# A Perceiver block on one core: the attention's output is regrouped without transposes and divided on its regrouped rows, sums and norms become stages of their own, and the last down product is made of two fp32r products

## The reference

```python
dot = jnp.einsum('bhsd,bhtd->bhst', Q, K) / np.sqrt(D_HEAD)
scores = jax.nn.softmax(dot, axis=-1)
out = jnp.einsum('bhst,bhtd->bhsd', scores, V)
out = out.reshape(B, T_src, D_MODEL)          # (head, s, d) as it lies: a row of 256 is 16 values of s of one head
return out @ Wh.T + bh
...
x = x + xattn(layernorm(x), ctx, ctx)
x = x + attn(layernorm(x))                    # divided by max(den, 1e-06)
x = x + ffn(layernorm(x))                     # silu(gate) * up, then down; weights are int32 / 127
```

## Time and profile before

| | |
|---|---|
| runs | 875.84, 876.47, 878.09 us (median 876.47) |
| profiled execution | 875.48 us, its span 873.8 us, so 1.7 us lie around the span |
| TensorE busy | 829.1 us (95%) |
| ScalarE, VectorE busy | 541.5 us (62%), 417.2 us (48%) |
| granted TensorE clock, mean | 0.99 of full |
| last batch's tail, alone at the end | from 796.97 us of the span on |

### The profile page before, as it was taken

One profiled execution on the slowest core, in us unless ns is written; L12 is line 12 of the kernel. 1 busy time (PEld: TensorE's weight loads), 2 busy tenths in 40 slices (PEclk: granted clock), 3 DMA queues, 4 the chain that ended last, 5 costly groups with the idle time before them and its releaser, 6 DMA issues.

```text
span 873.8 us, 20543 instructions
## 1 busy us (share of the span) xinstructions
PE 829.1 (95%) x8817; PEld 569.8 (65%) x8817; DVE 417.2 (48%) x746; ACT 541.5 (62%) x598; POOL 47.1 (5%) x76
## 2 busy tenths in 40 slices
PE   6899999999999998999999998999999999989876
PEld 5666666666666666676666665667666666657656
DVE  7433236444644445534654446354474444402654
ACT  2478887776577665667567764575657666672141
POOL 1034000000000000000000000000000000000010
PEclk9899999999999999999999999999999999999999
DMA  7486654646344333346343441443614333202000
GB/s 248 172 258 237 241 183 166 209 158 193 122 146 146 142 125 133 122 133 191 136 146 145 146 142 53 158 158 129 195 65 170 122 122 119 100 2 50 0 2 15
DMA packets 58768, 120.08 MB, mean 137 GB/s; under 512 B 21552, under 2 KB 29744, under 8 KB 55152
## 3 DMA queue, kind: packets, MB, share of 16 engines
q1 hardware_dynamic: 56880, 114.31, 38.3%
q0 software_dynamic: 1792, 4.40, 1.7%
HBM read 78.84 MB, written 37.75 MB: 133 GB/s over the span
## 4 chain that ended last, share of the span: by engine, by line
PE 82%; DVE 8%; issue 4%; DMA 2%; ACT 2%; DVEq 1%; POOL 1%; SPq 0%; POOLq 0%; ACTq 0%
PE ps_o L816 26%; PE ps_s L828 18%; PE ps_pa L662 10%; PE ps_pa L617 10%; PE ps_pa L763 2%; PE ps_pa L692 2%; PE ps_pa L788 2%; PE ps_pa L775 2%; PE ps_pa L754 1%; ACT probs L1258 1%; PE ps_pa L740 1%; DMA oscr<-y 1%; PE ps_pa L684 1%; PE ps_pa L795 1%; PE ps_pa L767 1%
## 5 line engine op out<-in xcount | busy, mean ns | idle before, releaser
L1258 ACT ACTIVATE probs<-ps_s 128x1024 f32<-128x1024 f32 x512 | 496.8, 1023 | 234.2 <-PE ps_s L828 227.7
L816 PE MATMUL ps_o<-probs,values 128*17 128x256 f32 x4096 | 256.1, 385 | 0.0
L828 PEld LDWEIGHTS ps_s<-qstack,kstack 64*128 64x128 f32 x2048 | 140.0, 186 | 99.6 <-ACT probs L1258 48.8
L828 PE MATMUL ps_s<-qstack,kstack 64*128 64x256 f32 x2048 | 194.0, 307 | 5.3 <-ACT probs L1258 5.3
L816 PEld LDWEIGHTS ps_o<-probs,values 128*17 128x17 f32 x4096 | 104.1, 98 | 98.7 <-issue 9.8
L1343 DVE TENSOR_SCALAR kparts<-ps_pa,b_heads 128x512 fp32r<-128x512 f32 x64 | 48.0, 750 | 107.4 <-PE ps_pa L617 107.1
L662 PE MATMUL ps_pa<-wv_hi,ctx_hi 128*128 128x256 f32 x256 | 79.6, 311 | 2.9 <-DVE wv_lo L1331 2.2
L1360 DVE TENSOR_TENSOR values<-ps_pa,bv_pair 128x512 f32<-128x512 f32 x64 | 44.2, 690 | 77.5 <-PE ps_pa L662 77.1
L662 PE MATMUL ps_pa<-wv_lo,ctx_hi 128*128 128x256 f32 x256 | 72.5, 283 | 0.0
L662 PE MATMUL ps_pa<-wv_hi,ctx_lo 128*128 128x256 f32 x256 | 72.4, 283 | 0.0
L617 PE MATMUL ps_pa<-ctx_hi,wk_hi 128*128 128x512 f32 x128 | 56.4, 441 | 0.0
(11 more groups left out here) (274 smaller groups left out, 786.7 us busy)
## 6 DMA issues: line engine op xcount, KB each, us to landing
kstack<-kscr SPq DMA_DIRECT2D x96, 512.0 KB, 5.3
kscr<-kparts SPq DMA_DIRECT2D x64, 512.0 KB, 2.7
ctx_raw<-ctxT SPq DMA_DIRECT2D x32, 512.0 KB, 6.5
qstack<-qscr SPq DMA_DIRECT2D x12, 256.0 KB, 3.5
qscr<-qparts SPq DMA_DIRECT2D x4, 512.0 KB, 3.1
xh<-x SPq DMA_DIRECT2D x4, 256.0 KB, 5.4
kstack<-kstack SPq DMA_DIRECT2D x2, 512.0 KB, 6.0
qstack<-ksample SPq DMA_DIRECT2D x4, 256.0 KB, 3.6
```

The source lines that it names most:

```text
L816: last = mm(ps_o[32 * j:32 * j + DH + 1, g * S:(g + 1) * S], values[par][:, i, head_of_step(g, j), :], prob[:, j * S:(j + 1) * S], start=b ...
L828: last = mm(ps_s[s % 2][:, j * S:(j + 1) * S], kstack[par][rows, u, i * P:(i + 1) * P], queries[rows, u, :], start=True, stop=True)
L1258: nc.scalar.activation(probs[n % AHEAD][:, :], ps_s[n % 2][:, :], ACT.Exp, scale=float(DH) ** -0.5).then_inc(fast["exp_done"], 1)
```

## The change

1. `o` alone is left on the way: `write_heads` writes each of the four 17-partition pieces of o_sb to memory by a DMA of its own (rows of 1 KB, denominators too), with no transpose before it. `read_rows` reads them back in pieces of 64 bytes as rows of 16 successive s of one head, all 17 of them, into o_rows (a view of feat). A new VectorE stage `on` takes the reciprocals, checks the denominators and divides into y.
2. `ln1` and `ln2` are stages of their own, for VectorE alone: `wh` and `wout` give their signal behind the sum.
3. At the end two of the four writes are issued from ScalarE; the check of the denominators and its verdict stand later; `last_down` takes hid in two fp32r parts, which VectorE cuts (`cut`).
4. The down weights are held as fp32r; before the end they are read as fp32, as before. They are loaded by two DMAs.

```diff
-AT = {"o": 1, "oT0": 3, "oT1": 4, "yT": 12, "wh": 13, "ln1T": 19, ...
+AT = {"o": 1, "on": 9, "yT": 12, "wh": 13, "ln1": 13, "ln1T": 19, ...
-      ... "o2T1": 88, "y2T": 90, "wout": 92,
+      ... "o2T1": 88, "y2T": 90, "wout": 92, "ln2": 92,
...
-            "powered": (["ln0"], ["wh", "wout"]),
+            "powered": (["ln0"], ["ln1", "ln2"]),
...
-        oscr = scratch("oscr", [H, S, DH], FP32)
+        oscr = scratch("oscr", [ST, DH + 1, HALF, S], FP32)
...
+        def write_heads(eng, c, j):
+            t, e = j // CI, j % CI
+            eng.dma_start(oscr[t].rearrange("d (g e) s -> e d g s", e=CI)[e],
+                          o_sb[32 * j:32 * j + DH + 1, :, :]).then_inc(c["o_written"], 16)
...
-                wait_all((c["operand"], c.at("operand", clock, "oT1")))
-                for t in range(ST):
-                    sp.dma_start(oscr[:, t * P:(t + 1) * P, :].rearrange("h s d -> s h d"),
-                                 y[:, t, :].rearrange("p (h d) -> p h d", h=H)).then_inc(c["o_written"], 16)
+                wait_all((c["operand"], c.at("operand", clock, "o")))
+                for j in range(GH):
+                    write_heads(sp, c, j)
+            def read_rows(t, landed):
+                sp.dma_start(o_rows[:, t, :, :], oscr[t].rearrange("d h (a u) -> (h a) d u", u=DH)).then_inc(landed, 16)
             def regroup_output(c, tails):
-                wait_all((c["o_written"], tails * 32 + 32))
-                sp.dma_start(y[:, :, :], oscr.rearrange("(t a) (u s) d -> (a u) t (s d)", t=ST, u=S // DH)
-                             ).then_inc(c["o_in"], 16)
+                wait_all((c["o_written"], tails * (16 * GH) + 16 * GH))
+                for t in range(ST):
+                    read_rows(t, c["o_in"])
...
-            for t in range(ST):
-                sp.wait_ge(*vector_of(f"y{t}"))
-                sp.dma_start(oscr...)
-            sp.wait_ge(fast["o_written"], B * 32)
+            sp.wait_ge(*vector_of("o0"))
+            sp.wait_ge(*scalar_of("o1"))
+            for j in range(CI):
+                write_heads(sp, fast, j)
+            sp.wait_ge(fast["o_written"], B * (16 * GH))
...
                 for t in range(ST):
-                    last = mm((ps_p, ps_a)[t][:, 0:D], hid[:, k, t * P:(t + 1) * P], wd_sb[:, k, :],
-                              start=k == 0, stop=k == HB - 1)
+                    for part in range(2):
+                        last = mm((ps_p, ps_a)[t][:, 0:D], last_part(k, part)[:, t * P:(t + 1) * P], wd_r[:, k, :],
+                                  start=k + part == 0, stop=k + part == HB)
...
+            warm(ps_p, 34)
+            for t in range(ST):
+                pe.wait_ge(*vector_of(f"y{t}"))
+                turn_rows(halves[2 + t], t, y).then_inc(last_product, 1)
...
+                elif name == "on":
+                    dve.wait_ge(c["o_in"], clock[1] * (16 * ST) + 16 * ST)
+                    if c is fast and tails:
+                        dve.wait_ge(c["stored"], tails * 16)
+                    v.reciprocal(rden[:, :, :], o_rows[:, :, DH, :])
+                    check_rows()
+                    for t in range(ST):
+                        last = scaled_rows(t)
...
                 elif name in ("wh", "wout"):
-                    v.tensor_tensor(xs[:, :, :], xs[:, :, :], bank[:, :].rearrange("p (t d) -> p t d", t=ST), ALU.add)
-                    dve.drain()
+                    last = v.tensor_tensor(xs[:, :, :], xs[:, :, :], bank[:, :].rearrange("p (t d) -> p t d", t=ST), ALU.add)
+                elif name in ("ln1", "ln2"):
                     last = layernorm(c, name, clock)
...
-                v.scalar_tensor_tensor(hid[:, k, :], gate_e[:, k % 2, :], 1.0, hid[:, k, :], ALU.add, ALU.mult
-                                       ).then_inc(last_vector, 1)
+                v.scalar_tensor_tensor(hid[:, k, :], gate_e[:, k % 2, :], 1.0, hid[:, k, :], ALU.add, ALU.mult)
+                dve.drain()
+                if k >= HALF // 2:
+                    dve.wait_ge(*product_of(f"gu{HB - 1}"))
+                cut(last_part(k, 0), last_part(k, 1), hid[:, k, :]).then_inc(last_vector, 1)
```

More of the change, by code:

```diff
@@ L1178, in _ @@
             pool.wait_ge(fast["k_stacked"][1], 3 * STACKED)
-            pool.dma_start(wd_sb[:, :, :].bitcast(INT32), wr(wdT)).then_inc(i_in, 16)
+            for k, part in zip((0, HB - CI), wd_int):
+                n = part.shape[1]
+                pool.dma_start(part, wr(wdT)[:, k:k + n, :]).then_inc(i_in, 16)
             def weighted(c, f, clock):
@@ L1286, in _ @@
                                  ).then_inc(last_scalar, 1)
+            act.wait_ge(*vector_of("o0"))
+            act.wait_ge(*scalar_of("o1"))
+            for j in range(CI, GH):
+                write_heads(act, fast, j)
             last_columns("yT1", "yT1", halves[3])
@@ L1412, in normalise @@
-                by_half = bank[:, :].rearrange("p (g a e c) -> p a g e c", a=CI, e=CI, c=32)
-                scale = rden[:, :].rearrange("p (g a e) -> p a g e", a=CI, e=CI)
-                for a in range(CI):
-                    last = v.tensor_tensor(y[:, t, a * P:(a + 1) * P].rearrange("p (g e d) -> p g e d", e=CI, d=DH),
-                                           by_half[:, a, :, :, 0:DH],
-                                           scale[:, a, :, :].unsqueeze(3).to_broadcast([P, G, CI, DH]), ALU.mult)
@@ L1418, in normalise @@
-                return last
+                heads, scale = bank[:, :].rearrange("p (h c) -> p h c", c=32), rden[:, t, :]
+                v.tensor_scalar(scale, heads[:, :, DH], floor, None, ALU.max)
+                dve.drain()
+                v.reciprocal(scale, scale)
+                dve.drain()
+                return v.tensor_tensor(y[:, t, :].rearrange("p (h d) -> p h d", d=DH), heads[:, :, 0:DH],
+                                       scale.unsqueeze(2).to_broadcast([P, H, DH]), ALU.mult)
@@ new lines, in scaled_rows, with check_rows @@
+            def scaled_rows(t):
+                return v.tensor_tensor(y[:, t, :].rearrange("p (u d) -> p d u", d=DH), o_rows[:, t, 0:DH, :],
+                                       rden[:, t, :].unsqueeze(1).to_broadcast([P, DH, DH]), ALU.mult)
+            def check_rows():
+                den, kept = o_rows[:, :, DH, :], den_in[:, 0, :].rearrange("p (t u) -> p t u", t=ST)
+                same = den_in[:, 1, :].rearrange("p (t u) -> p t u", t=ST)
+                v.tensor_scalar(kept, den, DEN_LEAST, DEN_MOST, ALU.max, ALU.min)
+                dve.drain()
+                v.tensor_tensor(same, kept, den, ALU.is_equal)
+                dve.drain()
+                v.tensor_reduce(den_ok[:, 1:2], den_in[:, 1, :], AX.X, ALU.min)
+                dve.drain()
+                v.tensor_tensor(den_ok[:, 0:1], den_ok[:, 0:1], den_ok[:, 1:2], ALU.min)
+                dve.drain()
@@ L1624, in setup_tail @@
                     v.tensor_copy(wu_r[:, k, :], wu_int[k])
-                v.tensor_copy(wd_sb[:, :, :], wd_sb[:, :, :].bitcast(INT32))
+                for k, part in zip((0, HB - CI), wd_int):
+                    v.tensor_copy(wd_r[:, k:k + part.shape[1], :], part)
                 dve.drain()
@@ L1713, in _ @@
             dve.wait_ge(fast["stored"], (B - 1) * 16)
[L1714 to L1728 removed]
             dve.wait_ge(fast["x_in"], B * 16)
             add_bias(bh_sb)
+            for t, landed in enumerate(((fast["o_in"], (B - 1) * (16 * ST) + 16), (o_in_last, 16))):
+                dve.wait_ge(*landed)
+                v.reciprocal(rden[:, t, :], o_rows[:, t, DH, :])
+                dve.drain()
+                scaled_rows(t).then_inc(last_vector, 1)
+            last_columns("yT0", halves[2])
+            check_rows()
+            dve.sem_inc(judged, 1)
+            last_norm("wh", "var1")
             dve.wait_ge(judged, 2)
```

112 lines of the change are left out of this document (25 added, 87 removed), and 2 rows, old and new, of the table AT.

## The result

The changed kernel takes 925.81 us in the median (925.17 to 927.26, 4 runs) against 877.28 us (875.84 to 879.27, 4 runs) for the kernel before: a ratio of 1.0554, 95% interval 1.0527 to 1.0581, slower by 48.5 us. The prediction was 930 us, slower. The profiled execution of the changed kernel took 927.26 us, its span is 925.5 us; that of before took 875.48 us.

The account below looks back on a forecast made before the run. TensorE, with 82% of the chain, was taken as the bound, so its stalls are paid in full. 46.5 - 8.0 + 9.2 + 0.3 + 3.0 + 0.4 + 2.3 = +53.7 us on 875.5; median 930 us, range 871 to 945.

Parts of the forecast that it names:

- The writes with 17 rows: Four output writes, 272 KB in all: all on one DMA engine at 21.3 KB per us, 13.1 us; chance 0.72.
- The tail in the middle: Three tails: yT starts at 222.7 instead of 210.22, a 12.5 us stall each; with clock falls +46.5 us.
- The fall of the clock: TensorE's clock drops to nearly all 1.2 GHz behind each of the three stalls, costing 3.0 us each.
- Norms apart: ln0T in two batches: waits of 2.33 and 2.68 us and a 3.0 us clock fall go, -8.0 us.
- The end: Last tail, nothing beside it: yT +9.2 us, second half's division +0.3, clock fall +3.0, verdict +0.4.
- the second half: At the end, its division comes ahead of the copy of the first half's columns: +0.3 us.
- The verdict's +0.4: At the end, the verdict's two short instructions stand ahead of the second copy: 0.5 at most, taken as +0.4 us.
- Down in fp32r: Last feed-forward part: VectorE's added cast and subtraction make it the bound, 1.83 us a block; +2.3 us net.
- the shorter last product: Last down product: two fp32r products instead of four passes, 0.5 in place of 0.74 us until L1794 starts.
- the queues of SyncE and ScalarE do not add up: End's writes from two issuers share one engine, so 13.1 us stand; if apart, 6.5 us less, whole 923.
- The sum: Whole kernel: all terms together +53.7 us on the profiled execution's 875.5, median forecast 930 us.
- The writes are spread: Rival: 17 rows shared over the engines, yT +0.8 us a batch, together -3.7, 873 us; chance 0.22.

Follow-up runs that it names:

- norms apart: The kernel before with only ln1 and ln2 as stages of their own and wh and wout signalling behind their sum: 874.03 us, ratio 0.9957.
- experiment 8: The changed kernel with all four writes of the end issued by SyncE, none by ScalarE: 925.53 us, ratio 1.0551 to the kernel before.
- experiment 3: The kernel before with only the norms ln1 and ln2 made stages of their own: 874.03 us, ratio 0.9957 to the kernel before.
- experiment 7: The changed kernel with 76 identity products in place of 34 ahead of the end's turned rows: 922.81 us, ratio 1.0551 to the kernel before.
- experiment 4: The changed kernel with the end's down in one plain fp32 product and no cut: 924.42 us, ratio 1.0512 to the kernel before.
- experiment 9: Second measurement of the kernel before with only ln1 and ln2 as stages of their own: 874.39 us over 9 runs, ratio 0.9963.
- the twelfth kernel: The changed kernel with each 17-row write cut into one of 16 rows and one of 1: 884.78 us, ratio 1.0089 to the kernel before.

## Why the prediction was right, point by point

**The writes with 17 rows: right, and the size too.** Two facts show the one engine: one packet beyond the data for each write, and the 0.07 of 16 engines while they run. That the count's divisors decide is shown by the series 17, 18, 19, 32 at the same code: 926, 887, 931, 887 us. The Trainium skill (DMA: Bandwidth & Descriptors, section Why a DMA increments its semaphore by 16 and not by 1) gives the rule, the largest number up to 16 that divides the slowest dimension of both sides, those of size 1 left out; the trace agrees, down to the 9 engines for 18 rows. I had put 13.1 us for the four from the kernel's mean rate per engine, 21.3 KB per us; at the end the reads went out 14.50 us behind the first write, where 0.4 + 13.1 + 0.8 = 14.3 was the sum's. No run shows the 0.4 and the 0.8 each by itself; the 14.50 leave 1.4 us for the two together.

**The tail in the middle: the wait right, the clock too dear.** Landing of the writes behind the copy: 20.6 us, against 20.3 in the prediction. The stretch from the copy to yT grew by 12.2, 11.2 and 11.3 us in the three tails, 34.7 in sum, where 3 x 12.5 = 37.5 was counted. The fall of the clock came behind each stall, but cost 2.6, 1.7 and 1.4 us in place of 3.0 each, 5.8 for 9.0:

| tail | wait for y | granted clock, 6.8 us from yT on | from yT to ln1T's first product |
|---|---|---|---|
| norms apart, 1 / 2 / 3 | 0 / 0.64 / 0.56 | 1.00 each | 8.41 / 8.38 / 8.39 |
| changed, 1 | 13.16 | 0.59 | 11.05 |
| changed, 2 | 12.96 | 0.73 | 10.08 |
| changed, 3 | 12.99 | 0.78 | 9.81 |
| 18 rows, 1 | 2.89 | 0.75 | 10.01 |
| 18 rows, 2 | 3.92 | 0.61 | 10.94 |
| 18 rows, 3 | 4.12 | 0.56 | 11.24 |

What each tail lost is near the share of the clock that was missing, times 6.8 us (2.8, 1.8 and 1.5 in the changed kernel), and so it is put down to the clock; no run has these tails at full clock. So the tails cost 40.5 us and not 46.5. Against norms apart alone the three batches are 15.1, 12.4 and 15.8 us longer, 43.4 in sum, and most of what lies between 40.5 and 43.4 is not the change's: the batch with the third tail is 12.7 us late at ln1T and still at the gates' fourth block, 136 us later, and loses 3.1 more at the fifth and sixth, where its clock was 0.76 (801 to 808) and 0.72 (819 to 825). The execution of experiment 8, the same program in the middle, has a clock of 1.00 in both places and loses nothing there.

**Norms apart: right in sign, half the size.** The step that failed was "both waits go, and the fall behind the second with them": -8.0. They go, and two others of 4.4 us in sum take their place; -3.1 to -3.8 us was measured, -4.1 by the copies of the two batches (experiment 3). I had said that nothing else moves later, and nothing did. But TensorE moved earlier, to the next things that VectorE has to deliver.

**The end.** yT +8.0 us in place of +9.2: the writes were as predicted, the reads landed in 3.4 us (the median for feat<-oscr on the page of the profile) and not in 4.0 like the old writes. From yT to the norm's rows +2.4 us, 8.11 against 5.69, of which the clock is 1.8 (experiment 7); the other 0.6 is there at full clock too (6.31 us in experiment 7 and with 18 rows). The prediction had 3.0 for the clock and 0.3 for the second half. The verdict's +0.4 did not show: from the norm's rows to the rows of the second output, the stretch in which it now stands, are 34.6 us, 34.9 before. Down in fp32r +2.1 (2.3), shown by experiment 4; the block took 1.72 us and not 1.83, since the next block's first instruction starts 0.08 before the subtraction's record ends (910.90 against 910.56 + 0.42) and not 0.02 behind. The 0.24 that the shorter last product was to give back did not show: VectorE waited 0.89 us for it, and 0.79 before. Together +12.1, against +15.2.

That the queues of SyncE and ScalarE do not add up, left open between 6.5 us and nothing, is settled by experiment 8. The Trainium skill (DMA: Bandwidth & Descriptors, section Issuing engines are not separate DMA queues) says so, and the trace agrees.

**The sum.** +53.7 us were predicted on the profiled execution, and +51.8 came (927.26 - 875.48). By the table: the tails 3.1 less than counted, the end 3.1 less, norms apart 2.3 more (-5.7 over the three batches in this execution of it, -4.5 in that of experiment 9), and 2.0 more ahead of the first copy, where the prediction had nothing and where executions of one kernel differ as much. So the sum was nearer than its terms, and partly by luck: the falls of the clock late in the batch with the third tail and the 2.0 us ahead of the first copy are not shown to come from the change. Without them the stretches give 40.5 for the tails, -4.1 for norms apart and +12.1 for the end, together +48.5, which is also what the medians differ by (that they agree to the tenth is chance). Measured so, the sum was 5 us too high: 6.0 in the tails and 3.1 at the end, less the 3.9 by which the gain of norms apart was too large.

**The rivals.** "The writes are spread", 873 us, had the mechanism wrong for 17 rows, and its price is wrong too: where they are spread, with 18, 32 or 16 + 1 rows, the kernel takes 885 to 887 us. It had counted 0.8 us of wait in each tail, and there are 3 to 4, with a fall of the clock behind that costs 1.6 to 2.8 more.

## What to carry to other kernels

Before a DMA is given a new shape, look at the number of its rows: a prime count of 17 puts it on one engine at some 21 KB per us, while 18, or 16 and 1, took 39 to 41 of the 48 us off here. A round trip through memory that other work just covers (15 us from the copy to yT here) leaves no room: with 18 rows it came 2 us later, and a fall of the clock doubled that. Read first how much slack the old way had, to the microsecond. And where a wait is taken away, ask which one the freed engine meets next.

## What the runs showed of the hardware that was not expected

- More bytes cost nothing where more engines share them: 18 rows are 72 KB on nine engines and 32 rows 128 KB on sixteen, 8 KB on each in both, and the kernels take 886.9 and 887.5 us.
- The one-row write of the twelfth kernel is not on one engine. ScalarE's queue has 176 packets, 2 x 88; with 64 + 16 for the 16 rows and 4 data packets of 1 KB for the one, 4 are left for engines. So it looks as if the next dimension, the four pieces of 1 KB, were shared out.
- A short wait of TensorE brings the clock down too, and the price does not follow the length of the wait. Behind waits of 2.89, 3.92 and 4.12 us in the 18-row kernel the way to ln1T took 1.6, 2.6 and 2.8 us longer; behind waits of 13 us in the changed kernel 2.6, 1.7 and 1.4.
- A fall can also come in one execution and not in the next of the same program: late in the batch with the third tail the norms-apart kernel had none in experiment 3 and one in experiment 9 (190.8 and 192.2 us). It is worth some 1.5 us and has to be taken out before two traces are compared.
